# Cross-attention and expert layer on one core: constant products on TensorE in three places of the opening, and three early steps at other places in their queues

## What is computed

```
q = Wq @ layernorm(x) + bq;   k = Wk @ ctx + bk;   v = Wv @ ctx + bv        (256 x 512 each)
x = x + softmax_over_keys(mask * q.k / 4 - (1 - mask) * 1e6) * mask @ v      (16 heads of 16)
x = x + shared_down(sigmoid(shared_gate y) * shared_up y)                    (y = layernorm(x))
      + sum over the top 2 of 8 experts of weight * expert(y) in bf16
```

## Time and profile before

| What | Value |
|---|---|
| median of three runs | 656.15 us (655.79 to 662.23) |
| profiled execution, span | 651.7 us |
| median over that span | 4.4 us more |
| TensorE busy | 606.6 us, 93% of the span |
| DVE / ACT / POOL busy | 507.6 / 472.0 / 360.0 us |
| chain that ended last, share of TensorE | 76% |
| first score product starts | 35.03 us after the start of the span |

### The profile page before, as it was taken

The page is one execution under the profiler, slowest core; times in us unless marked ns, Lnnn a source line. Parts: engine busy times, 40 slices in busy tenths (PEclk is TensorE's granted clock), DMA queues, the critical chain, the costliest instruction groups (busy, mean ns, idle before and its releaser), DMA issues.

```text
span 651.7 us, 12576 instructions
## 1 busy us (share of the span) xinstructions
PE 606.6 (93%) x4110; PEld 259.2 (40%) x4110; DVE 507.6 (78%) x970; ACT 472.0 (72%) x662; POOL 360.0 (55%) x494
## 2 busy tenths in 40 slices
PE   4799999999999999999999999879999999999987
PEld 4543333333333333333333332224554466666532
DVE  2479899999999999999999999964528654454577
ACT  3654899899899899899898888985432276667511
POOL 5559453684684684684684462251553577777310
PEclk9899999999999999999999999999999999999999
DMA  8642434534525535534433432115698533333178
GB/s 293 195 135 76 114 93 145 168 110 144 170 87 168 167 89 171 167 112 146 135 111 102 132 111 80 50 52 121 170 220 184 110 105 106 100 106 107 50 230 310
DMA packets 64990, 88.66 MB, mean 136 GB/s; under 512 B 12624, under 2 KB 45264, under 8 KB 63904
## 3 DMA queue, kind: packets, MB, share of 16 engines
q1 hardware_dynamic: 60032, 68.72, 34.4%
q0 software_dynamic: 4896, 19.14, 12.1%
HBM read 63.75 MB, written 32.74 MB: 148 GB/s over the span
## 4 chain that ended last, share of the span: by engine, by line
PE 76%; DVE 11%; issue 6%; ACT 5%; DMA 1%; POOL 1%; SPq 0%; ACTq 0%; DVEq 0%; POOLq 0%
PE PS L1083 17%; PE PS L986 11%; PE PS L1311 9%; PE PS L1055 8%; PE PS L1774 7%; DVE MX L996 7%; PE PS L845 5%; PE PS L1837 4%; PE PS L1585 4%; ACT E L1069 2%; PE PS L840 2%; PE PS L991 1%; PE PS L933 1%; PE PS L1732 1%; PE PS L929 1%
## 5 line engine op out<-in xcount | busy, mean ns | idle before, releaser
L996 DVE TENSOR_REDUCE MX<-PS 128x1 f32<-128x512 f32 x512 | 323.1, 683 | 17.3 <-PE PS L986 15.4
L1069 ACT ACTIVATE E<-PS 128x1024 f32<-128x1024 f32 x256 | 253.5, 1020 | 32.7 <-PE PS L1055 28.6
L986 PE MATMUL PS<-BIG 53*128 53x512 f16 x512 | 128.6, 384 | 12.2 <-DVE MX L996 10.8
L1083 PE MATMUL PS<-E,BIG 128*32 128x512 f32 x1024 | 136.4, 605 | 2.0 <-ACT E L1069 2.0
L1055 PE MATMUL PS<-BIG 55*128 55x512 f16 x512 | 101.2, 381 | 8.2 <-ACT E L1069 3.5
L879 POOL TENSOR_TENSOR ML<-BIG,ML 128x512 f32<-128x512 f32 x30 | 38.3, 1277 | 102.8 <-ACT BIG L855 102.6
L986 PEld LDWEIGHTS PS<-BIG 53*128 53x128 f16 x512 | 34.3, 93 | 134.0 <-DVE MX L996 120.1
L1796 DVE SCALAR_TENSOR_TENSOR E<-WP,PS 128x352 bf16<-128x352 f32 x39 | 20.3, 521 | 47.0 <-ACT WP L1786 47.0
L1774 PE MATMUL PS<-BIG,CT 128*128 x312 | 53.0, 313 | 1.8 <-DVE WP L1346 1.0
L855 ACT ACTIVATE BIG<-PS,BIG 128x256 f32<-128x256 f32 x64 | 35.7, 560 | 25.9 <-PE PS L840 14.5
L1856 POOL DMA_INDIRECT scr_ys<-SW,bvB x39 | 38.3, 981 | 20.8 <-DVE SW L1849 12.5
(11 more groups left out here) (261 smaller groups left out, 904.0 us busy)
## 6 DMA issues: line engine op xcount, KB each, us to landing
scr_parts<-WP SPq DMA_DIRECT2D x96, 128.0 KB
BIG<-scr_parts SPq DMA_DIRECT2D x64, 192.0 KB
BIG<-in_we POOLq DMA_DIRECT2D x8, 1088.0 KB, 14.1
scr_u<-ML SPq DMA_DIRECT2D x32, 256.0 KB, 3.0
X<-in_x SPq DMA_DIRECT2D x8, 512.0 KB, 6.5
CT<-in_ctx SPq DMA_DIRECT2D x8, 512.0 KB, 4.1
ML<-scr_u SPq DMA_DIRECT2D x16, 256.0 KB
ML<-scr_recs SPq DMA_DIRECT2D x16, 256.0 KB
```

The lines of the kernel that those rows point to most:

```text
L986: e.matmul(PS[:, yi[name] % 3, :], QK[rows, qb(u), 0, j0 + jj, 128 * tt:128 * tt + 128], QK[rows, qb(u), 1, j0 + jj, :], start=True, stop= ...
L996: e.tensor_reduce(MX[:, g % 2, c:c + 1], PS[:, yi[name] % 3, :], AX.X, ALU.max)\
L1069: e.activation(E[:, st, 2 * jj:2 * jj + 2, :], PS[:, slot(name):slot(name) + 2, :], ACT.Exp, scale=1 / 1024).then_inc(s["rc"], 1)
L1083: ins = e.matmul(PS[32 * hh:32 * hh + 32, AVB, :], VT[:, b % 2, st, 4 * (g % 4) + hh, :], E[:, st, hh, :], start=(st == 0), stop=(st == 3))
```

## The change

It adds a step `keep_clock(n)`: TensorE issues n constant products like those of line 991 into bank 7 (once the constant identity is there). It stands at three places of TensorE's queue: 28 products at -20, ahead of everything; 14 at -1.2755, behind q's products of unit 1; 8 at -0.995, ahead of the first score product. The four steps of `split_shared` get other places: ACT's squares -0.95 (were -1.9), TensorE's sum with DVE's fetch and POOL's factors -0.72 (-1.26), ACT's scaling and upper halves -0.6 (-0.95), POOL's lower halves -0.55 (-0.9). The row load of batch 2 goes from -1.98 to -1.5.

```diff
--- before.py
+++ after.py
@@ -268,7 +268,7 @@
             tv = -1 - .25 * IT if w == 1 else w - 2 + 0.65 * IT
             mring += [(tv, ("v", w, 0)), (tv + (.1 if w == 1 else 1.0499999999999998) * IT, ("v", w, 1))]
         mring.append((-3 + 3.6 * IT, ("w",)))
-        mring.append((-1.26, ("z",)))
+        mring.append((-.72, ("z",)))
         mring.append((.5537, ("wz",)))
         for b in range(B):
             mring.append((2 * b - 3 + 3.7 * IT if b == 0 else 2 * b - 4 + 5.8 * IT, ("f", b)))
@@ -327,7 +327,7 @@
                 e.dma_start(TM[:, b, :], m8[b:b + 1].broadcast_to([8, 16, 32])).then_inc(s["tm"], 16)
         sp.at(0.3, load_tm)
         for b in range(2, B):
-            sp.at(2 * b - 6 + .02, load_x(b))
+            sp.at(-1.5 if b == 2 else 2 * b - 6 + .02, load_x(b))
 
         sp.at(-20, sp_setup)
         sp.at(-18, load_one)
@@ -514,6 +514,16 @@
 
         DA = -0.05 * IT
 
+        def keep_clock(n):
+            def mm(e):
+                e.wait_ge(s["id"], 6)
+                for _ in range(n):
+                    e.matmul(PS[:, AVB, 0:256], identb[:, :], ident[:, :].bitcast(BF), start=True, stop=True)
+            return mm
+        pe.at(-20, keep_clock(28))
+        pe.at(-1.2755, keep_clock(14))
+        pe.at(-.995, keep_clock(8))
+
         def weight_norms():
             name = ("w",)
             bank = yi[name] % 3
@@ -762,7 +772,7 @@
                 for i, (v, o, _, _) in enumerate(cells):
                     ins = e.activation(o, v, ACT.Square, accum_out=ZS[:, i:i + 1])
                 ins.then_inc(s["zq"], 1)
-            act.at(-1.9, squares)
+            act.at(-.95, squares)
 
             def mm(e):
                 take_bank(e, name)
@@ -793,7 +803,7 @@
                 e.wait_ge(s["zt"], 1)
                 for v, o in full:
                     e.activation(o, v, ACT.Copy).then_inc(s["zh"], 1)
-            act.at(-.95, upper)
+            act.at(-.6, upper)
 
             def lower(m):
                 def f(e):
@@ -802,7 +812,7 @@
                         e.wait_ge(s["nm"], 1)
                     n = sizes[m]
                     e.tensor_tensor(outs[m][:, n:2 * n], STG[m], outs[m][:, 0:n], ALU.subtract).then_inc(s["sw"], 1)
-                pool.at(-.9, f)
+                pool.at(-.55, f)
             for m in range(3):
                 lower(m)
 
```

## The result

The changed kernel takes 669.14 us (median of 4 executions, 662.88 to 677.93) against 657.09 us (4 executions, 655.79 to 662.23): 1.56% slower, ratio 1.0156 with a 95% interval of 1.0097 to 1.0214. The forecast was 654.9 us and "the same"; the time lies outside the range and on the other side. (All ratios here leave out the slow executions, those over 1.5% above the quickest of the same kernel; the medians of all four alone give 1.0183.)

The account below looks back on a forecast made before the run. It took TensorE, busy 93% of the span, as the main bound; -3.1 (start) + 1.5 (ring slot wait) + 0.3 = -1.3 us against the median 656.15 gave 654.9 us, "the same" (chance 0.95), range 651.7 to 657.8.

Parts of the forecast that it names:

- 28 products at the head: Ahead of the weights' sums: full clock shortens these by 1.3 to 1.7 us, 1.5 taken; nothing waits behind the products.
- rival 4: Clock falls again while TensorE idles 3.4 us between q and k; k's split up to 1.5 us later; 656.3 us, chance 0.05.
- The reciprocal: DVE's step at the end of the DVE and POOL chain before the score products: moves from 33.54 to 32.05 us.
- The loads: SP's loads of unit 0's k, with batch 2's row load behind them: first score product between 31.0 and 33.3 us.
- The start's gain: Opening up to the second score product, 32.6 against 35.78 us: gain 3.1 us, 3.3 at best, 1.7 without the sums' gain.
- The constant products themselves fill idle time: Up to 30.8 us, ahead of the first score product: they only fill time in which TensorE waits for the loads anyway.
- the pace of the first group: Group 0's score products: set by TensorE, 0.75 us for one score product with three constant ones, as before.
- The ring slot of line 1032: Turned maxima of group 0: TensorE waits 1.45 us for ACT's fetch of unit 2's q, behind the shared weights' steps.
- The upper price of 2.5 us: Most that the ring slot wait was taken to cost when setting the chances of over 1% faster or slower.
- The sum: All terms together: -3.1 + 1.5 + 0.3 = -1.3 us on the span.
- the range's upper end: 657.8 us: a start without gain, its full wait and the spread of the two lower runs.

Follow-up runs that it names:

- bridge38: The changed kernel with 38 instead of 8 constant products ahead of the first score product: 661.32 us, ratio 1.0051 to the kernel before.
- changed_3: The changed kernel run again unaltered, on the second of the two slower chips: 704.95 us, ratio 1.0145 to the kernel before.
- filled: The kernel before, first score product held until POOL has split k of unit 1, TensorE running 50 constant products meanwhile: 668.01 us.
- best: The same kernel as zearly_fill, once more on another chip: 655.10 us, ratio 0.9969 from four executions, two others at 669.82 and 674.73.
- no_warm: The kernel before without its own constant products in groups 0 and 1 (WARM (3, 1) to (0, 0)): 658.62 us, ratio 1.0045.
- head_only: The kernel before with only the 28 constant products at the head: 655.13 us, ratio 0.9960 from seven of ten executions.
- gap_idle: The kernel before, first score product held until POOL has split k of unit 1, TensorE idling meanwhile: 681.83 us.
- cover56: zearly_fill with 56 instead of 38 constant products ahead of the first score product: 689.70 and 693.18 us on two slower chips, ratios 1.0023 and 0.9984.
- zearly_fill: bridge38 with the shared weights' sum after 4 instead of 10 score products and 26 constant products between unit 0's q and k: 653.16 us, ratio 0.9958.

## Why the prediction was wrong

- **28 products at the head**: "the weights' sums take 2 us instead of 3.6": 1.95 us in the row above, right, and nothing waited for the products.
- **q to k**: rival 4 said the clock might fall in the gap there. It did, at 16.16, and k's eight pieces took 3.54 us. The reciprocal came at 32.93, forecast 32.05. The half microsecond that the weights landed earlier than before hides part of that.
- **The loads**: first score product at 32.65 in a forecast range of 31.0 to 33.3; second at 33.49 against 32.6. The start's gain is 2.3 us, forecast 3.1. SP's loads of k began at 27.26, against 30.38, so the later row load did what it was to do.
- **"The constant products themselves fill idle time: at 30.8 TensorE still waits for the loads."** This is the step that failed. The wait was seen and given the price nothing. TensorE was through at 29.7, and the idle 2.94 us cost the clock for 47.8 us, some 19 us at 0.40. The trace of before had shown a fall only after 3.4 us of idling, and no fall after the 1.34 us ahead of k, so the forecast looked for a fall only where a gap was about 3.4 us long (rival 4). Gaps of 1.1, 1.3, 1.6 and 2.9 us came before falls in these profiles. Rival 4's own argument, that a head start followed by a gap costs the clock, fitted this gap too and was not applied to it.
- **"From there the pace of the first group is TensorE's, 0.75 us … as before."** It was 1.29. The prediction had no fall there, and its only measures of a return were 3.8 us of q and 6.8 us of k and v. Score products of 53 rows with three constant ones between are another kind of busy.
- **The ring slot of line 1032**: in this profile it was hidden, because TensorE itself was late. At full clock it shows, 1.28 us against a forecast of 1.45 (bridge38, and the changed kernel itself in changed_3). Mechanism and size were right; the clock behind it was left out. The upper price of 2.5 us for this wait, which the chances use, stands in no run; the two profiles in which the wait shows have 1.28.
- **The sum**: -1.3 us; at equal clock the fits give -2.1, with an error too large to confirm it. What the sum lacked was one term, the price of idling, and no rival held it: rival 4 named the fall but at another place and for 1.5 us. The Trainium skill (TensorE: Matmul & The Clock Gate, "What's actually happening") puts the ramp to full clock at under 1% of a typical kernel's span. What this trace shows is not such a ramp but a clock that doesn't come back for 48 us, and it costs 14 us, over 2%.
- **Two slips that change nothing**: the 20.3 us of the earlier trace rows are waits of the weight loads' queue (PEld); the products themselves idle only 4.6 of those 66 us. And the range's upper end, from its own terms (656.15 + 1.45 + 0.36), is 658.0, not 657.8.

## What to carry to other kernels

An idle microsecond of TensorE isn't priced by its own length alone, but also by what TensorE runs next: ahead of the fp32 projections a wait of 2.13 us cost no clock and one of 3.4 us cost 6.8 us at half clock, while waits of 1.1 to 7.1 us among the score products, where the clock fell and three or one constant products stood between them, brought 10 to 51 us of it. So when work ahead of a wait gets faster, or a step moves out of it, fill the wait with constant products and a margin (56 where 38 mostly did), or leave it as busy as it was. And look at the clock of several executions, not of the profiled one alone: a mean clock 0.01 lower was 5 us here.

## What the runs showed of the hardware that I had not expected

- Most of the scatter is the clock. Over 49 executions of the kernel before on three chips, 652.5 to 660.2 us, the span follows half-clock time at 0.40 us for each us, and the line accounts for 78% of the variance.
- Short waits can be enough: after 1.28 us (bridge38), 1.63 us (filled) and 1.13 us (best) the clock fell, and in no_warm after none longer than 0.57 us; after 0.67 and 0.88 us (head_only) it didn't, nor after 1.04 us in the changed kernel's last profile. What decides between them was not tried.
- A TensorE that is busy throughout can stay at half clock for 47.8 us (the changed kernel's profile); in gap_idle it was 51.2 us, of which it idled the first 2.2. With eight constant products for each score product the stretch was 3.4 and 6.8 us.
- The clock can fall while TensorE runs one-column fp32 products: in cover56's first profile they begin at 8.20, right behind constant products at full clock, and it falls near 10.2, 2 us into them; in zearly_fill at 10.19, 0.9 us into them and 1.20 us of waiting. It stayed at half through the rest of them and q.
- Chips differ by stage: on two of five the same program takes 688 and 695 us instead of 657; the kernels profiled there have half-clock stretches in the experts' stage, from about 530 us on. Why was not looked into.
